# Forming the remainders of the down projection and of Wx on VectorE in place of GpSimd

## The chip, the cores and the metric

The kernel runs on one core of a Trainium2 chip. The metric is the device time of one execution in microseconds (us), lower is better. The engines of the core are TensorE (PE, and PEld for its weight loads), VectorE (DVE), ScalarE (ACT), GpSimd (POOL) and SyncE (SP), which here only issues transfers.

## The reference

Two layers, each added to its input. The first is a low-rank adaptation conditioned on `cond`; the second is a tanh recurrence over the time axis.

```
c   = layernorm(cond) * gamma + beta
w   = gelu(c @ W1 + bias1) @ W2 + bias2           # 16 x 16384
a1, b1, a2, b2 = split(w, 4)                      # each 16 x 512 x 8
u   = x . a2 ;  mid = gelu(x @ base_down + u . b2)
v   = mid . b1 ; out = mid @ base_up^T + v . a1
x   = x + (x + out)                               # B=16, T=512, D=512
xW  = x @ Wx + b
h_t = tanh(xW_t + h_{t-1} @ Wh)                   # h_0 = cond, 512 steps
y   = x + h
```

## The kernel before, in words

Matrix products of fp32 data are made from two rounded parts. A matrix W is held as `W[HI]`, W rounded to fp32r, and `W[LO]`, the remainder W - W[HI] rounded in turn; a product of two such matrices takes three passes (HI HI, HI LO, LO HI). ScalarE forms each HI part by a copy and another engine forms the LO part by a subtraction. For W2, up, x, mid and x1 that other engine is VectorE. For the down projection (`down_s`) and for Wx (`wx_s`) it is GpSimd (line L462): two instructions of 128x2048 elements in the whole kernel.

The work has three parts.

1. Start (about 0 to 28 us): layer norm, W1, the scale of Wh (`scl`), and the first weights. SyncE loads 1 MB pieces into a ring of four slots of the buffer `work`: entries 0 and 1 are up and down, entries 2 to 33 are the 32 half tiles of W2, entry 34 is Wx. Entry 4 waits until TensorE has turned up (`up_tr`), entry 5 goes into the slot of down and waits for `w_split` 1, the remainder of down. Entry e from 6 on waits until VectorE has formed the remainder of the W2 tile that lay in its slot (`w2_lo`). SyncE's queue is in order, and the loads of x for chunk 0 (`load_x`, L412) stand between entries 5 to 8.
2. Stream (about 28 to 176 us): `STREAM` = 39 steps written out by hand on each engine. In step i ScalarE rounds W2 tile i+2 (L489), VectorE forms the remainder of tile i (`w2_low`, L689), TensorE multiplies tile i with the hidden vector (L907), and the result is turned into the factors a1, b1, a2, b2. The tables `PE_FILL`, `ACT_FILL` and `DVE_FILL` put pieces of the first chunk's dense work between (`dense_slot(0, r)`).
3. Chunks: time is cut into 16 chunks of 32 steps. `chunk(c)` runs the recurrence (TensorE L944, VectorE L804 to L812, ScalarE L593) and interleaves the dense work of chunk c+1 and the first part of chunk c+2. Before chunk 0 the function `run_chunks` runs the last part of chunk 0's dense work: xw, the product with Wx, 48 matmuls of 512 columns in slots 24 to 31, together with the first part of chunk 1: VectorE transposes x (L728), ScalarE rounds it (L544), VectorE forms its remainder (L736).

The first xw matmul waits for `w_split` 2, the remainder of Wx (L995). The xw order takes for output tiles m=0 and m=1 first k = 0 to 2 (items 0 to 17), then k = 3 (from item 18). Item 0, 3, 6 and 18 wait for the remainder of x1 of k = 0, 1, 2, 3 (`x1lo_done`, VectorE L766), which follows `x1` (VectorE L761) and its rounding by ScalarE (L561). The first `down_s` matmul waits for `w_split` 1 (L962).

In VectorE's stream the second of these x1 (k=1) and the remainder k=0 stand in step 35, x1 of k=2 and the remainder of k=1 in step 36, the remainder of k=2 in step 37, x1 of k=3 in step 38. After the stream come the transposes of k=0 and k=1 of chunk 1, then the remainder of x1 k=3. ScalarE's order there is: x1 rounding k=0, Wx rounding (L583, step 35), x1 rounding k=1 and k=2, rounding of x k=0 and k=1 of chunk 1, x1 rounding k=3.

```
            for n, (src, dst) in enumerate(((down_f, down_s), (wx_f, wx_s))):
                pool.wait_ge(w_hi, n + 1)
                nc.gpsimd.tensor_tensor(dst[:, LO], src, dst[:, HI].bitcast(F32), ALU.subtract).then_inc(w_split, 1)
```

GpSimd's only other work behind these two is the sum of x1 and h, once per time step of the recurrence (L469).

Of the kernel before, what the change touches and what calls it, by code (L numbers as in the profile page):

```python
# [6 lines left out]
F32 = mybir.dt.float32  # L7
# [3 lines left out]
ALU = mybir.AluOpType  # L11
# [14 lines left out]
HI, LO = 0, 1  # L26
# [81 lines left out]
FIRST_TAIL = 24  # L108


WH_HI_AT, WH_LO_AT, WX_HI_AT = 0, 1, 35


def build(nc: bass.Bass, x, cond, down, up, gamma, beta, w1, bias1, w2, bias2, wx, wh, b, y):
# [13 lines left out]
    with ExitStack() as ctx:  # L128
        def sb(name, shape, dt=F32):
            return ctx.enter_context(nc.sbuf_tensor(name, shape, dt))  # L130
# [4 lines left out]
        def sem(name):  # L135
            return ctx.enter_context(nc.semaphore(name))


        down_s = sb("down_s", [P, 2, KT, D], F32R)
        up_s = sb("up_s", [P, 2, KT, D], F32R)  # L140
        wx_s = sb("wx_s", [P, 2, KT, D], F32R)
# [17 lines left out]
        up_f, down_f, wx_f = [work[:, s, :].rearrange("p (k n) -> p k n", k=KT) for s in range(3)]  # L159
# [76 lines left out]
        w_hi = sem("w_hi")  # L236
        w_split = sem("w_split")
# [112 lines left out]
        def plan(rank, first, shares):  # L350
            items = dense_items(KT, rank)
            parts = portions([1 if p >= 0 else 0.5 for _, _, p in items], shares)
            return stage_plan(items, {first + n: range(*part) for n, part in enumerate(parts)})
# [88 lines left out]
        @block.gpsimd  # L442
        def _(pool):
            nc.gpsimd.memset(ident[:], 0.0).then_inc(pool_set, 1)
            nc.gpsimd.memset(mask_b[:], 1.0).then_inc(pool_set, 1)
            pool.wait_ge(pool_set, 2)
            nc.gpsimd.affine_select(out=ident[:], in_=ident[:], compare_op=ALU.not_equal, fill=1.0, base=0,
                                    pattern=[[-1, P]], channel_multiplier=1).then_inc(pool_set, 1)

            for rep in range(REPS):  # L450
                m = mask_b[:, rep, :]
                base = -rep * GB * RANK
                nc.gpsimd.affine_select(out=m, in_=m, compare_op=ALU.is_ge, fill=0.0, base=base,
                                        pattern=[[-RANK, GB]], channel_multiplier=1).then_inc(pool_set, 1)
                pool.wait_ge(pool_set, 4 + 2 * rep)
                nc.gpsimd.affine_select(out=m, in_=m, compare_op=ALU.is_ge, fill=0.0, base=RANK - 1 - base,
                                        pattern=[[RANK, GB]], channel_multiplier=-1).then_inc(pool_set, 1)


            for n, (src, dst) in enumerate(((down_f, down_s), (wx_f, wx_s))):  # L460
                pool.wait_ge(w_hi, n + 1)
                nc.gpsimd.tensor_tensor(dst[:, LO], src, dst[:, HI].bitcast(F32), ALU.subtract).then_inc(w_split, 1)  # L462

            for c in range(NC):
                pool.wait_ge(x1lo_done, (c + 1) * KT)
                for t in range(TC):
                    pool.wait_ge(h_done, 2 * (c * TC + t) + 2)
                    xs = x1[c % 3].rearrange("p k (b t) -> p k b t", t=TC)[:, :, :, t]
                    nc.gpsimd.tensor_tensor(xs, xs, hf[:, t % 4], ALU.add).then_inc(sum_done, 1)  # L469
# [139 lines left out]
        def _(dve):  # L609
# [73 lines left out]
            def w2_low(n):  # L683

                dve.wait_ge(w2_hi, n + 1)
                if w2_prev[n] >= 0:
                    dve.wait_ge(row_mm, w2_prev[n] + 1)
                dst = w2_s[n].rearrange("p s k n -> p s (k n)")
                nc.vector.tensor_tensor(dst[:, LO], w2_raw(n), dst[:, HI].bitcast(F32),  # L689
                                        ALU.subtract).then_inc(w2_lo, 1)  # L690

            def split_up(k):

                src = bulk[:, BANK_UP[k], :]
                dve.wait_ge(up_hi, k + 1)
                nc.vector.tensor_tensor(up_s[:, LO, k], src, up_s[:, HI, k].bitcast(F32),
                                        ALU.subtract).then_inc(up_split, 1)

            def factor(n):

                q, dt = W2_TILES[n]
                f = fac[:, n % 2]
                dve.wait_ge(fac_mm, n + 1)
                if n == 0:
                    dve.wait_ge(small_in, 64)
                if n >= 2:
                    dve.wait_ge(fac_split, n - 1)
                nc.vector.tensor_reduce(fsum[:], rec[:, n % 2, 0:RANK * 2 * B].rearrange(
                    "p (r s b) -> p r b s", r=RANK, s=2), AX.X, ALU.add).then_inc(fsum_done, 1)
                dve.wait_ge(fsum_done, n + 1)  # L710
                pw = fsum[:].rearrange("p r (g b) -> p g b r", g=GROUPS)
                bias = bias2T[:, q, dt:dt + 1, :].rearrange("p (o a) r -> p o a r", o=1).broadcast_to([P, GROUPS, GB, RANK])
                for rep in range(REPS):
                    last = nc.vector.tensor_tensor(f[:, :, rep], pw, bias, ALU.add)
                last.then_inc(fac_done, 1)

            def split_factor(n):

                src, dst = factor_views(n)
                dve.wait_ge(fac_hi, n + 1)  # L720
                nc.vector.tensor_tensor(dst[:, LO], src, dst[:, HI].bitcast(F32), ALU.subtract).then_inc(fac_split, 1)
# [47 lines left out]
            def turn_y(c, k):  # L769

                if k == 0:
# [2 lines left out]
                nc.vector.transpose(yn[:, c % 2, :, k, :], x1[c % 3][:, k].rearrange(  # L774
                    "p (b t) -> p b t", t=TC)).then_inc(y_done, 1)

            for k in range(KT):
                split_up(k)
            for i in range(STREAM):
                if i < HALVES:  # L780
                    w2_low(i)
                if i % 2 == 0 and 0 <= i // 2 - 3 <= LAST:
                    split_factor(i // 2 - 3)
                if i % 2 == 0 and 0 <= i // 2 - 2 <= LAST:
                    factor(i // 2 - 2)
                if i == WH_LO_AT:
                    dve.wait_ge(wh_hi, 1)
                    nc.vector.scalar_tensor_tensor(out=wh_s[:, 1], in0=wh_f, scalar=w_scale, in1=wh_s[:, 0],
                                                   op0=ALU.mult, op1=ALU.subtract).then_inc(wh_split, 1)
                for r in DVE_FILL.get(i, ()):  # L790
                    dense_slot(0, r)

# [35 lines left out]
        def _(pe):  # L828
# [93 lines left out]
            def dense(stage_plan, i, banks, w_s, src, rank_f, done):  # L922

                items, _, starts, ends, _ = stage_plan
                m, k, p = items[i]
                if p >= 0:
                    a, w = PASSES[p]
                    mm = nc.tensor.matmul(bulk[:, banks[m], :], w_s[:, w, k, m * P:(m + 1) * P], src[:, a, k, :],  # L928
                                          start=(i in starts), stop=(i in ends), skip_group_check=True)
                else:  # L930
                    mm = nc.tensor.matmul(bulk[:, banks[m], k * GC:(k + 1) * GC],  # L931
                                          rank_f[:, -1 - p, k, m * P:(m + 1) * P], rank_s[:, k * GC:(k + 1) * GC],
                                          start=False, stop=(i in ends), skip_group_check=True)
                if i in ends:
                    mm.then_inc(done, 1)
# [125 lines left out]
```

## Time and profile before

| what | value |
|---|---|
| median of 3 runs | 1312.95 us (1311.94 to 1314.33) |
| the profiled execution | 1311.74 us |
| its span in the trace | 1310.0 us |
| TensorE | busy 1258.5 us, 96% of the span |
| VectorE, ScalarE, GpSimd busy | 990.0, 701.6, 288.9 us |
| mean granted TensorE clock | 0.972 of 2.4 GHz |

The span lies within the execution; 1.7 us of the profiled execution are outside it. Busy shares are averages over the three parts, which have different limits.

### The profile page before, as it was taken

The numbers are of one execution on the slowest core, as the hardware profiler recorded it, in microseconds if no ns is written. First come the engines' busy times: TensorE is split into PE (matmuls) and PEld (weight loads), VectorE is DVE, ScalarE is ACT, GpSimd is POOL, SyncE is SP. The second block draws the span as 40 slices with busy tenths as digits, with TensorE's granted clock in tenths as the row PEclk, the third lists the DMA queues.
The fourth block names the chain that finished last, engine by engine and source line by source line (L and its number), as shares of the span: only waits on it lengthen the run. The fifth ranks groups of instructions, "written<-read, shape, count | busy, mean of one in ns | idle before, by whom it ended". The sixth has DMA issues, their size and how long they took to land.

```text
span 1310.0 us, 49303 instructions
## 1 busy us (share of the span) xinstructions
PE 1258.5 (96%) x20280; PEld 1021.1 (78%) x20280; DVE 990.0 (76%) x3723; ACT 701.6 (54%) x2497; POOL 288.9 (22%) x525
## 2 busy tenths in 40 slices
PE   6698989999999999999999999999999999999996
PEld 6264578888888888888888888888888888888764
DVE  6679757777777878787878787777778787877664
ACT  4566635555555555555555555555555555555542
POOL 1000012222222222222222222222222222222111
PEclk6798889999999999999999999999999999999998
DMA  7888720121212122121312121212121221102022
GB/s 256 227 290 279 203 33 10 27 38 31 35 27 35 27 35 35 27 43 19 51 19 45 24 43 27 38 31 35 27 34 27 35 35 27 27 3 35 2 35 34
DMA packets 292271, 75.63 MB, mean 58 GB/s; under 512 B 273072, under 2 KB 273088, under 8 KB 292048
## 3 DMA queue, kind: packets, MB, share of 16 engines
q1 hardware_dynamic: 285680, 71.89, 24.7%
q8 instruction: 160, 2.62, 0.8%
q10 hardware_dynamic: 6368, 0.60, 0.4%
q14 instruction: 63, 0.52, 0.1%
HBM read 55.68 MB, written 16.78 MB: 55 GB/s over the span
## 4 chain that ended last, share of the span: by engine, by line
PE 85%; ACT 2%; DVE 2%; issue 0%; POOL 0%; DVEq 0%; POOLq 0%; ACTq 0%
PE bulk L928 43%; PE rec L944 31%; PE bulk L917 5%; PE bulk L931 5%; ACT hf L593 1%; PE bulk L907 1%; DVE z L804 1%; ACT rec L534 1%; PE rec L894 0%; POOL wx_s L462 0%; DVE work L774 0%; DVE wx_s L689 0%; ACT wx_s L583 0%; DVE hs L812 0%; DVE hs L809 0%
## 5 line engine op out<-in xcount | busy, mean ns | idle before, releaser
L944 PEld LDWEIGHTS rec<-hs,wh_s 128*128 128x128 f16 x16352 | 442.5, 96 | 129.0 <-DVE hs L812 126.4
L593 ACT ACTIVATE hf<-z,scl 128x32 f32<-128x32 f32 x1024 | 273.8, 315 | 482.4 <-DVE z L804 478.2
L944 PE MATMUL rec<-hs,wh_s 128*128 128x32 f16 x16352 | 493.2, 177 | 7.3 <-ACT rec L534 7.3
L469 POOL TENSOR_TENSOR work<-work,hf 128x64 f32<-128x64 f32 x512 | 278.4, 544 | 842.7 <-DVE hs L812 842.7
L804 DVE TENSOR_REDUCE z<-rec 128x32 f32<-128x96 f32 x1022 | 231.0, 256 | 111.1 <-PE rec L944 97.7
L809 DVE TENSOR_SCALAR hs<-hf 128x32 f16<-128x32 f32 x1024 | 181.5, 177 | 106.2 <-ACT hf L593 106.2
L812 DVE SCALAR_TENSOR_TENSOR hs<-hf,hs 128x32 f16<-128x32 f32 x1024 | 197.2, 193 | 35.3
L928 PE MATMUL bulk<-act_x,down_s 128*128 128x512 f32 x768 | 217.4, 406 | 2.1 <-ACT mid_s L556 2.1
L928 PE MATMUL bulk<-mid_s,up_s 128*128 128x512 f32 x768 | 218.8, 408 | 0.0
L928 PE MATMUL bulk<-act_s,wx_s 128*128 128x512 f32 x768 | 208.8, 409 | 3.5 <-POOL wx_s L462 3.5
L534 ACT ACTIVATE rec<-work 128x32 f32<-128x32 f32 x1022 | 183.7, 210 | 0.0
L928 PEld LDWEIGHTS bulk<-act_s,wx_s 128*128 128x128 f32 x768 | 136.7, 191 | 26.4 <-POOL wx_s L462 3.7
L928 PEld LDWEIGHTS bulk<-act_x,down_s 128*128 128x128 f32 x768 | 131.8, 188 | 20.4 <-ACT mid_s L556 2.3
L928 PEld LDWEIGHTS bulk<-mid_s,up_s 128*128 128x128 f32 x768 | 132.2, 189 | 17.6
L566 ACT ACTIVATE work<-bulk,bs,scl 128x512 f32<-128x512 f32 x64 | 48.1, 776 | 24.2 <-PE bulk L928 23.8
L728 DVE STREAM_TRANSPOSE work<-work 128x512 f32<-128x512 f32 x64 | 44.8, 703 | 7.5 <-DMA work<-in_x_dram 7.5
L766 DVE TENSOR_TENSOR act_s<-work,act_s 128x512 fp32r<-128x512 f32 x64 | 47.6, 745 | 1.9 <-ACT act_s L561 1.9
L931 PE MATMUL bulk<-rank_s,b_s 128*128 128x256 f32 x256 | 45.6, 292 | 0.0
L931 PE MATMUL bulk<-rank_s,a_s 128*128 128x256 f32 x256 | 45.6, 292 | 0.0
L757 DVE TENSOR_TENSOR mid_s<-gel,mid_s 128x512 fp32r<-128x512 f32 x64 | 43.8, 684 | 2.2 <-ACT mid_s L556 2.2
L761 DVE SCALAR_TENSOR_TENSOR work<-work,bulk 128x512 f32<-128x512 f32 x64 | 43.6, 681 | 2.3 <-PE bulk L931 0.9
L774 DVE STREAM_TRANSPOSE work<-work 128x512 f32<-128x512 f32 x64 | 44.7, 703 | 0.7 <-POOL work L469 0.5
(121 smaller groups left out, 971.4 us busy)
## 6 DMA issues: line engine op xcount, KB each, us to landing
work<-in_L_cond_W_dram SPq DMA_DIRECT2D x33, 1024.0 KB, 6.1
work<-in_x_dram SPq DMA_DIRECT2D x256, 64.0 KB, 3.4
out_dram<-work SPq DMA_DIRECT2D x248, 64.0 KB, 2.4
work<-in_L_cond_Wh_dram SPq DMA_DIRECT2D x1, 1024.0 KB, 5.4
work<-in_L_cond_base_up_dram SPq DMA_DIRECT2D x1, 1024.0 KB, 10.7
work<-in_L_cond_base_down_dram SPq DMA_DIRECT2D x1, 1024.0 KB, 13.2
work<-in_L_cond_Wx_dram SPq DMA_DIRECT2D x1, 1024.0 KB, 7.6
out_dram<-work ACTq DMA_DIRECT2D x8, 64.0 KB, 3.2
```

What stands on the lines that cost most here:

```text
L469: nc.gpsimd.tensor_tensor(xs, xs, hf[:, t % 4], ALU.add).then_inc(sum_done, 1)
L534: nc.scalar.activation(R[f][:, :, PARTS, :], xw[:, c % 2].rearrange("p k (b t) -> p k b t", t=TC)[:, f * HT:(f + 1) * HT, :, t], ACT.Copy) ...
L566: nc.scalar.activation(xw[:, n % 2, m], bulk[:, BANK_XW[m], :], ACT.Identity, bias=bs[:, m:m + 1], scale=fwd).then_inc(xw_done, 1)
L593: nc.scalar.activation(hf[:, t % 4, half], z[:, half], ACT.Tanh, scale=inv).then_inc(tanh_done, 1)
L766: nc.vector.tensor_tensor(act_s[:, LO, m], x1[n % 3][:, m], act_s[:, HI, m].bitcast(F32), ALU.subtract).then_inc(x1lo_done, 1)
L804: nc.vector.tensor_reduce(z[:, half], R[f].rearrange("p m j b -> p m b j"), AX.X, ALU.add).then_inc(z_done, 1)
L809: nc.vector.tensor_scalar(hs[:, half, 0, :], hf[:, t % 4, half], H_SCALE, None, ALU.mult).then_inc(hi_done, 1)
L812: nc.vector.scalar_tensor_tensor(out=hs[:, half, 1, :], in0=hf[:, t % 4, half], scalar=H_SCALE, in1=hs[:, half, 0, :], op0=ALU.mult, op1=A ...
L917: last = nc.tensor.matmul(bulk[:, out_bank, g * GC:(g + 1) * GC], fac_s[:, k, g, :], src[:, a, k, g * GC:(g + 1) * GC], start=(k == g == a ...
L928: mm = nc.tensor.matmul(bulk[:, banks[m], :], w_s[:, w, k, m * P:(m + 1) * P], src[:, a, k, :], start=(i in starts), stop=(i in ends), ski ...
L931: mm = nc.tensor.matmul(bulk[:, banks[m], k * GC:(k + 1) * GC], rank_f[:, -1 - p, k, m * P:(m + 1) * P], rank_s[:, k * GC:(k + 1) * GC], s ...
L944: last = nc.tensor.matmul(R[fo][:, m, 0:PARTS, :], wh_s[:, q, k, n * P:(n + 1) * P], hs[:, k, :, :], start=(m == k == q == 0), stop=(k == ...
```

## The change

GpSimd's loop over the two weights is taken out. VectorE gets the same two instructions. The one for down stands right before `split_up(0)`, so before the remainders of up and the whole stream; the one for Wx stands in step 36 of VectorE's stream (`WX_LO_AT`), behind the factor work of that step and ahead of x1 of k=2. Semaphores and their counts are unchanged.

```diff
-WH_HI_AT, WH_LO_AT, WX_HI_AT = 0, 1, 35
+WH_HI_AT, WH_LO_AT, WX_HI_AT, WX_LO_AT = 0, 1, 35, 36
...
-            for n, (src, dst) in enumerate(((down_f, down_s), (wx_f, wx_s))):
-                pool.wait_ge(w_hi, n + 1)
-                nc.gpsimd.tensor_tensor(dst[:, LO], src, dst[:, HI].bitcast(F32), ALU.subtract).then_inc(w_split, 1)
...
+            def split_weight(n, src, dst):
+
+                dve.wait_ge(w_hi, n + 1)
+                nc.vector.tensor_tensor(dst[:, LO], src, dst[:, HI].bitcast(F32), ALU.subtract).then_inc(w_split, 1)
+
+            split_weight(0, down_f, down_s)
             for k in range(KT):
                 split_up(k)
             for i in range(STREAM):
...
+                if i == WX_LO_AT:
+                    split_weight(1, wx_f, wx_s)
                 for r in DVE_FILL.get(i, ()):
                     dense_slot(0, r)
```

## Rows read from the trace of the kernel before

**Rows 1.** The page: the span, and the chain that ended last, by engine.

```profile
span 1310.0 us, 49303 instructions
...
PE 85%; ACT 2%; DVE 2%; issue 0%; POOL 0%; DVEq 0%; POOLq 0%; ACTq 0%
```

**Rows 2.** Stages: us, then busy time of each engine, clock, DMA share, GB/s.

```profile
240.00:1310.00 1070.00, 1053.07 (x18778) 877.93 (x18776) 817.51 (x3406) 570.78 (x2275) 267.58 (x492) 1.00 0.19 31
```

**Rows 3.** The chain that ended last, 172 to 193 us: start, us, what.

```profile
172.35 0.70 DVE work L761
...
173.69 1.82 ACT wx_s L583
175.58 4.53 POOL wx_s L462
180.15 12.46 PE bulk L928 x42
```

**Rows 4.** VectorE in order of time, 174 to 185 us (idle before in brackets).

```profile
174.66 0.68 DVE L761 SCALAR_TENSOR_TENSOR work<-work,bulk 128x512 f32<-128x512 f32 x1
176.05 5.19 DVE L766 TENSOR_TENSOR act_s<-work,act_s 128x512 fp32r<-128x512 f32 x2 [0.71 <-ACT act_s L561]
181.17 0.67 DVE L761 SCALAR_TENSOR_TENSOR work<-work,bulk 128x512 f32<-128x512 f32 x1
181.77 1.29 DVE L728 STREAM_TRANSPOSE work<-work 128x512 f32<-128x512 f32 x2
184.26 0.69 DVE L766 TENSOR_TENSOR act_s<-work,act_s 128x512 fp32r<-128x512 f32 x1 [1.21 <-ACT act_s L561]
```

**Rows 5.** VectorE in order of time, 21 to 54 us.

```profile
21.97 0.23 DVE L661 TENSOR_TENSOR h_s<-hT,h_s 128x64 fp32r<-128x64 f32 x1 [6.15 <-ACT h_s L496]
...
24.77 3.53 DVE L680 TENSOR_SCALAR z0s<-z0s,scl 128x64 f32<-128x64 f32 x1
...
28.35 2.47 DVE L696 TENSOR_TENSOR up_s<-bulk,up_s 128x512 fp32r<-128x512 f32 x4
...
53.64 0.71 DVE L728 STREAM_TRANSPOSE work<-work 128x512 f32<-128x512 f32 x1 [5.18 <-DMA work<-in_x_dram]
```

**Rows 6.** GpSimd in order of time, start of the kernel.

```profile
23.74 4.51 POOL L462 TENSOR_TENSOR down_s<-work,down_s 128x2048 fp32r<-128x2048 f32 x1 [21.35 <-ACT down_s L505]
```

**Rows 7.** Instructions on the tile wx_s: min/median/max ns, first and last start.

```profile
L689 DVE TENSOR_TENSOR wx_s<-work,wx_s x13: 2274/2284/2291, 39.8 to 159.4; 128x2048 fp32r<-128x2048 f32 x13
```

**Rows 8.** ScalarE in order of time, 26 us, and 175 to 184 us.

```profile
26.25 1.15 ACT L502 CAST up_s<-bulk 128x512 fp32r<-128x512 f32 x2
...
175.41 1.13 ACT L561 CAST act_s<-work 128x512 fp32r<-128x512 f32 x2
182.50 1.21 ACT L544 CAST act_x<-work 128x512 fp32r<-128x512 f32 x2 [5.96 <-DVE work L728]
183.62 0.61 ACT L561 CAST act_s<-work 128x512 fp32r<-128x512 f32 x1
```

**Rows 9.** SyncE's queue in order of time, 28 us.

```profile
28.69 3.29 SPq L412 DMA_DIRECT2D work<-in_x_dram  x4
```

**Rows 10.** Stage: us, clock, DMA share, GB/s.

```profile
28.00:30.00 2.00, 0.50 0.57 170
```

**Rows 11.** TensorE before the xw product, in order of time.

```profile
176.06 0.63 PE L931 MATMUL bulk<-rank_s,a_s 128*128 128x256 f32 x4
```

**Rows 12.** Stages, TensorE alone: us, busy (matmuls), clock, DMA share, GB/s.

```profile
180.15:185.80 5.65, 5.65 (x13) 0.50 0.13 21
185.80:192.40 6.60, 6.60 (x30) 1.00 0.63 100
```

**Rows 13.** Stages in and behind gaps of TensorE; columns as in rows 2.

```profile
126.00:128.06 2.06, 0.00 (x0) 0.00 (x0) 0.13 (x2) 2.06 (x5) 0.00 (x0) 1.00 1.00 368
142.70:145.19 2.49, 0.01 (x1) 0.01 (x1) 2.49 (x3) 1.03 (x2) 0.00 (x0) 0.93 0.66 249
145.20:148.26 3.06, 3.06 (x13) 1.67 (x14) 2.54 (x3) 2.57 (x3) 0.00 (x0) 0.50 0.63 172
```

## The prediction

> **What bounds the kernel now.** I read the page first, for its chain of work that ended last: 85% of it is TensorE [rows 1]. The stage view says where that holds: from 240 us to the end TensorE is busy 1053.07 of 1070 us at full clock [rows 2]. A change that touches nothing there moves the end by exactly as much as it moves the start of the recurrence, so the question is only what happens before the recurrence. There the chain in order of time has one place where TensorE is not the engine: ScalarE rounds Wx, GpSimd forms its remainder in 4.53 us, and the xw matmuls start as it ends, at 180.15 [rows 3]. TensorE's last matmuls before it end at 176.06 + 0.63 = 176.69 [rows 11], so it stands for 3.46 us.
>
> Next I read VectorE in order of time around both GpSimd instructions, looking for the same operation at another price. There are two. At 176.05 two remainders of 128x512 take 5.19 us together where the same operation takes 0.69 at 184.26; GpSimd works from 175.58 to 180.11 [rows 3, 4]. At 24.77 a scaling of 128x64 elements takes 3.53 us and ends at 28.30, where a subtraction of 128x64 takes 0.23; GpSimd's remainder of down ends at 23.74 + 4.51 = 28.25 [rows 5, 6]. I read both as VectorE held up until GpSimd's instruction is over. So each GpSimd instruction costs twice: its own length, and VectorE's time behind it.
>
> Last I read the granted clock. It is 0.50 from 180.15 to 185.80, in which 13 matmuls pass (0.43 us each), and 1.00 behind that, 30 to 31 in 6.60 us (0.213 each) [rows 12]. The fall came in the gap before 180.15: 1.2 GHz in place of 2.4.
>
> **The change, step by step.** The instruction itself is in the trace on VectorE: 13 remainders of the same shape, 2.28 us each [rows 7]. GpSimd's took 4.51 and 4.53 [rows 3, 6].
>
> *Down, at the start.* After the change VectorE's scaling at 24.77 finds GpSimd idle. I take 0.23 us, the 128x64 row; the ends are 0 and the 3.53 us of the row itself (rival C). With the small bias scaling behind it, priced at 0.1, VectorE is free at about 25.1. The remainder of down needs ScalarE's copy, done before 23.74 [rows 6], and runs from 25.1 to about 27.35. The remainders of up then start at 27.3 in place of 28.35 [rows 5]; ScalarE's last two copies of up end at 27.40 [rows 8] and the third remainder is not reached before 28.5, so nothing waits. Term: -1.05 us for everything behind VectorE: up, the first W2 remainders, the rows on TensorE, the scale of Wh.
>
> The second to wait for this is SyncE: entry 5 of the ring goes out with `w_split` 1, at 28.25 before [rows 6], the loads of x follow at 28.69 [rows 9]. It now goes at 27.35, 0.9 us earlier. Until 53.64 VectorE's transposes wait for these loads of x (5.18 us) [rows 5], so the term needs the transfers to move too. From 28 to 30 us the DMA engines are only 57% busy [rows 10]: they have room at the place where entry 5 arrives, so I take 0.9 to 1.05, call it 1.0. The other end is 0, if transfers set this part alone. From there to 174 us all engines wait for one another in the same order as before, and a shift carries through. TensorE's wait for `w_split` 1 at the first down matmul is long past. Nothing else stands in GpSimd's queue: its next work is the recurrence's sum.
>
> *Wx, at the end of the stream* (times of before, so without the shift). ScalarE's copy ends at 173.69 + 1.82 = 175.51 [rows 3]. VectorE reaches the new instruction at about 174.7, where x1 of k=2 began before [rows 4], stands 0.8 us, and runs it from 175.55 to 177.83. TensorE starts xw at 177.85, not 180.15: its gap is 1.16 us, not 3.46. Behind the new instruction in VectorE's queue stand x1 of k=2, the remainders of k=1 and k=2, x1 of k=3, two transposes and the remainder of k=3. With each at its row's price (0.68, 0.69, 0.67; starts follow 0.6 to 0.65 apart): x1 k=2 to 178.5, remainder k=1 to 179.1, ScalarE's copy of k=2 to 179.15, remainder k=2 to 179.85, x1 k=3 to 180.5. The transposes then start at 180.5 in place of 181.77, and from there to the end of the remainder k=3 it is 184.26 + 0.69 - 181.77 = 3.18 us, through ScalarE's three copies [rows 4, 8]: done at 183.7 in place of 184.95.
>
> TensorE: items 0 to 2 at 0.213 to 178.5; 0.6 us for k=1; items 3 to 5 to 179.8; items 6 to 17 from 179.9 to 182.45; 1.25 us for k=3; item 18 at 183.7. Before: 5.65 us at 0.43 is 13.2 items by 185.80, 4.8 more at 0.213 make 18 items at 186.8 [rows 12], later than the 184.95 at which k=3 was ready; the slow clock set it. Term: 183.7 - 186.8 = -3.1 us, if the clock stays up. Of this, 1.25 is the earlier remainder k=3 and 1.85 is the clock. Does it stay? A gap of 2.06 us passed with the clock at 1.00, one of 2.49 was followed by 0.50 [rows 13]. The new gaps are 1.16, 0.6, 0.1 and 1.25 us with work between. The nearest row is the one that stayed. If the clock falls all the same at about 180.1, 11 items at 0.43 end at 184.8, and some 2 us more at half speed cost 1.0: the term is -1.1. All that follows (the rest of xw, the first z) waits for TensorE, not for VectorE, whose work for chunk 1 ends 1.25 us earlier as well.
>
> **The sum.** -1.0 - 3.1 = -4.1 us against the profiled execution's 1311.74, so 1307.6. The median of the runs is 1312.95, 1.2 above that execution; nothing in the terms depends on which execution it is but the place where the clock changes. I predict the median: 1312.95 - 4.1 = 1308.8 us, 0.32% faster. A measurement of this kernel can tell about 0.2% (2.6 us) from no change.
>
> **The rivals.**
> *A, the clock falls in the split gap too.* For it: the row at 2.49 us, and the several waits within 6 us that together make 3.1. Against: the row at 2.06 and work between the waits. -1.0 - 1.1 = -2.1: 1310.8, within 0.2%.
> *B, the start gives nothing.* Transfers set the time to 53.64, and the ones of x keep their pace. For: the wait of 5.18 us; against: 57% at 28 to 30 us. -3.1 alone: 1309.8, just over 0.2% faster.
> *C, slower: VectorE's long instructions are long of themselves.* The 3.53 and the 5.19 us would then stay, and 2.28 us come on top. Start: the remainders of up begin at 30.6, +2.25. End: x1 k=2 to 178.5, the pair to 183.7, x1 k=3 to 184.3, transposes from there, remainder k=3 at 187.5, item 18 at 187.5 instead of 186.8, +0.7. Sum +2.95: 1315.9. It decides from the point where more than 2.3 us of the 3.53 are the instruction's own. Against: two different operations end with or right after GpSimd's, and the second has a row at 0.69.
> The Trainium skill, page "SBUF — State Buffer", section "Who interferes with whom", speaks to C: a VectorE instruction with two SBUF inputs, or in a two-port mode, and a GpSimd instruction exclude each other for the whole instruction, and the one that comes second is blocked. By that rule both long rows are waits and C falls; the trace agrees, with ends at 28.30 against 28.25. The same rule would speak against the change if GpSimd had other work beside the new instructions; it has none there.
> *D, before had less clock to lose.* Where the gap of 3.46 us leaves the clock up in the runs without a profile, the gain is -1.0 - 1.25 = -2.3: 1310.7.
>
> **Chances.** Forecast 0.62 (1307.3 to 1310.0 with the scatter of the runs shown, 1.2 us), B 0.14, A 0.12, D 0.08, C 0.04. Faster by over 0.2% (under 1310.3): most of the forecast, two thirds of B and a little of A and D, 0.71. Slower: C, 0.04. Within: 0.25. The range reaches from the forecast less the scatter and the earlier end of the terms, 1306.4, to A and D with some scatter, 1311.5.
>
> **What would show it.** VectorE's scaling at 24.8 at 0.2 to 0.3 us and no instruction of 128x512 over 1 us; the first up remainder about 1.05 us earlier; the last transposes of x at about 52.6; a TensorE gap of about 1.2 us before xw and three short waits in its first 18 items; clock 1.00 from there on; the first z of the recurrence about 4 us earlier than before, and the same length from there to the end. The prediction is wrong if the clock is 0.50 behind the gap, if the shift of the start is gone by 174 us, or if the span behind the first z changes.

## The result, and the profile after

The changed kernel takes 1308.87 us (median of 9 runs, 1307.43 to 1310.93); the kernel before, in 9 runs with it, 1314.62 us. The ratio is 0.9962, 95% interval 0.9952 to 0.9972: 5.0 us faster, between 3.7 and 6.3. The forecast was 4.1 us faster and 1308.8 us. The median of before shown ahead of the forecast (1312.95, three runs) lay 1.7 us under the later one. So the forecast of the time itself is met to 0.1 us by luck: the base was 1.7 us low and the gain 0.9 us small. What is to be compared is 4.1 with 5.0.

The profiled execution takes 1308.32 us. From its page, with rows 1 to compare:

```profile
span 1306.6 us, 49303 instructions
```

Start of VectorE's stream in the changed kernel, in order of time (compare [rows 5]):

```profile
25.89 0.16 DVE L675 COPY scl<-rec 128x3 f32<-128x3 f32 x1 [0.71 <-PE rec L880]
26.09 0.25 DVE L676 TENSOR_SCALAR z0s<-z0s,scl 128x64 f32<-128x64 f32 x1
...
26.39 2.29 DVE L776 TENSOR_TENSOR down_s<-work,down_s 128x2048 fp32r<-128x2048 f32 x1
28.59 2.48 DVE L692 TENSOR_TENSOR up_s<-bulk,up_s 128x512 fp32r<-128x512 f32 x4
...
54.13 0.71 DVE L724 STREAM_TRANSPOSE work<-work 128x512 f32<-128x512 f32 x1 [5.05 <-DMA work<-in_x_dram]
```

The scaling that took 3.53 us takes 0.25, the remainder of down 2.29. The first remainder of up starts 2.70 us after the copy of `scl`; before it was 28.35 - 24.58 = 3.77. That is 1.07 us less, where the forecast had 1.05. This execution is 1.3 us later than before at that copy, and the change is not the reason (last section), so times are counted from that copy from here on.

The chain that ended last, 172 to 190 us (compare [rows 3]):

```profile
172.67 0.70 DVE work L757
...
173.40 0.62 ACT act_s L557
174.02 1.82 ACT wx_s L579
...
175.86 2.29 DVE wx_s L776
178.15 0.61 DVE work L757
...
178.79 0.63 ACT act_s L557
...
179.44 0.69 DVE act_s L762
180.13 0.60 DVE work L757
180.73 0.64 DVE work L724
...
181.39 1.21 ACT act_x L540 x2
182.60 0.53 ACT act_s L557
...
183.15 0.70 DVE act_s L762
...
183.90 5.73 PE bulk L932 x24
```

Before, the chain went from GpSimd straight into 42 matmuls. Now the remainder of Wx is 2.29 us of it and the chain stays in VectorE's queue behind it: x1 of k=2, the remainder of k=2, x1 of k=3, the first transpose, ScalarE's three copies, the remainder of k=3. Only at item 18 does it enter TensorE. The lines left out are waits of at most 0.04 us. These are the steps of the forecast in their order.

TensorE there, and its stages (compare [rows 11, 12]):

```profile
176.40 0.63 PE L935 MATMUL bulk<-rank_s,a_s 128*128 128x256 f32 x4
178.21 0.96 PE L932 MATMUL bulk<-act_s,wx_s 128*128 128x512 f32 x3 [1.18 <-DVE wx_s L776]
179.41 3.79 PE L932 MATMUL bulk<-act_s,wx_s 128*128 128x512 f32 x15 [0.24 <-DVE act_s L762]
183.90 5.73 PE L932 MATMUL bulk<-act_s,wx_s 128*128 128x512 f32 x24 [0.69 <-DVE act_s L762]
```

```profile
178.20:183.90 5.70, 4.76 (x19) 1.00 0.08 13
183.90:189.60 5.70, 5.70 (x26) 1.00 0.63 100
```

The gap is 1.18 us in place of 3.46, the clock stays at 1.00 (2.4 GHz) through it and the small waits behind it, and the 24 matmuls from 183.90 on take 5.57 us, 0.23 each.

### The profile page after: what moved, and what is told of

It reads as the page before. It is cut to its first block, busy times and chain, and to the rows that moved or that the text cites. A ratio compares the mean times of both kernels' runs of the same rounds, so it can differ in the third digit from the quotient of the medians.

```text
span 1306.6 us, 49303 instructions
## 1 busy us (share of the span) xinstructions
PE 1257.4 (96%) x20280; PEld 1020.0 (78%) x20280; DVE 987.6 (76%) x3725; ACT 701.6 (54%) x2497; POOL 280.0 (21%) x523
## 4 chain that ended last, share of the span: by engine, by line
PE 90%; DVE 4%; ACT 3%; DMA 1%; issue 1%; SPq 0%; ACTq 0%; DVEq 0%; POOLq 0%; POOL 0%
PE bulk L932 43%; PE rec L948 31%; PE bulk L921 5%; PE bulk L935 5%; PE bulk L911 3%; ACT hf L589 1%; PE rec L898 1%; DVE act_s L685 1%; DVE z L808 1%; DMA work<-in_L_cond_W_dram 1%; ACT rec L530 1%; DVE wx_s L685 1%; PE rec L849 1%; PE bulk L867 1%; DMA work<-in_x_dram 0%
## 5 line engine op out<-in xcount | busy, mean ns | idle before, releaser
L562 ACT ACTIVATE work<-bulk,bs,scl 128x512 f32<-128x512 f32 x64 | 48.0, 775 | 22.1 <-PE bulk L932 21.8
L762 DVE TENSOR_TENSOR act_s<-work,act_s 128x512 fp32r<-128x512 f32 x64 | 43.8, 684 | 1.3 <-ACT act_s L557 1.2
```

The lines of the kernel that those rows point to most:

```text
L562: nc.scalar.activation(xw[:, n % 2, m], bulk[:, BANK_XW[m], :], ACT.Identity, bias=bs[:, m:m + 1], scale=fwd).then_inc(xw_done, 1)
```

## The experiments

One table holds what the traces say of all kernels, in us. The columns: from the copy of `scl` to the first remainder of up; from that copy to VectorE's fourth transpose of x, the last wait for transfers of the start; from that transpose to x1 of k=0; from there to the first z of the recurrence; from there to the end of the span. Then the ratio to the kernel before, run beside each of them, with its 95% interval.

| kernel | scl to up | scl to 4th transpose | to x1 | x1 to z | z to end | ratio |
|---|---|---|---|---|---|---|
| before | 3.77 | 29.06 | 118.71 | 23.93 | 1113.72 | 1 |
| changed | 2.70 | 28.24 | 118.54 | 20.63 | 1113.30 | 0.9962 (0.9952 to 0.9972) |
| e1 down only | 2.70 | 28.61 | 119.31 | 23.81 | 1114.08 | 0.9998 (0.9989 to 1.0007) |
| e2 Wx only | 3.79 | 28.85 | 122.04 | 20.64 | 1114.01 | 0.9976 (0.9966 to 0.9987) |
| e3 filled gap | 4.23 | 29.58 | 116.85 | 22.16 | 1114.22 | 0.9983 (0.9972 to 0.9995) |
| e4 Wx twice | 2.70 | 28.10 | 118.91 | 23.97 | 1113.39 | 0.9983 (0.9975 to 0.9992) |
| e5 GpSimd beside | 3.80 | 31.66 | 119.42 | 25.89 | 1113.89 | 1.0031 (1.0019 to 1.0043) |
| e6 x1 first | 2.69 | 28.16 | 118.92 | 19.86 | 1113.75 | 0.9955 (0.9943 to 0.9967) |
| e7 Wx early | 2.70 | 28.28 | 121.15 | 18.73 | 1113.76 | 0.9955 (0.9943 to 0.9967) |
| e8 changed again | 2.69 | 28.16 | 118.78 | 20.63 | 1113.34 | 0.9961 (0.9948 to 0.9973) |
| e9 down thrice | 7.35 | 33.28 | 121.05 | 20.62 | 1113.41 | 1.0010 (1.0001 to 1.0019) |
| e10 entry 5 late | 2.69 | 30.68 | 120.98 | 20.62 | 1113.92 | 0.9992 (0.9983 to 1.0000) |
| e11 down early | 0.50 | 28.52 | 118.73 | 20.63 | 1113.46 | 0.9973 (0.9964 to 0.9983) |
| e12 both early | 0.50 | 28.86 | 119.40 | 18.68 | 1113.74 | 0.9963 (0.9950 to 0.9977) |

The two rows of before that the table needs and that do not stand above, in VectorE's order of time:

```profile
24.58 0.16 DVE L679 COPY scl<-rec 128x3 f32<-128x3 f32 x1 [0.70 <-PE rec L876]
...
196.28 0.35 DVE L800 TENSOR_TENSOR z<-z0s,work 128x32 f32<-128x32 f32 x2 [7.73 <-ACT work L566]
```

The column x1 to z repeats to 0.01 us between kernels that have the same code there (20.62 to 20.64 in six of them). The column to x1 does not: 116.9 to 122.0 with the same code (e7 and e12 alone differ there, at its end). A microsecond is therefore read from its stage, and the ratios say only whether it arrived.

**e1, down alone.** The Wx loop stays on GpSimd:

```diff
-                if i == WX_LO_AT:
-                    split_weight(1, wx_f, wx_s)
...
+            pool.wait_ge(w_hi, 2)
+            nc.gpsimd.tensor_tensor(wx_s[:, LO], wx_f, wx_s[:, HI].bitcast(F32), ALU.subtract).then_inc(w_split, 1)
```

> Only the remainder of down is formed by VectorE; the remainder of Wx stays on GpSimd. The theory (GpSimd's instruction holds VectorE up, so VectorE's 2.28 us in place of 3.3 us of waiting gains 1.05 us, carried by the transfers): VectorE's scaling of 128x64 takes 0.25 us, the stretch from the copy of scl to x1 of k=0 is 1.0 us shorter than before, and the time is 1.0 us under the kernel before. The xw end is as before: the pair of remainders of k=1 and k=2 over 5 us, a TensorE gap of 3.4 us, the clock at 0.50 behind it. Rival, transfers set this part: 0 us. Rival, the 3.53 us are the scaling's own: 2.2 us more than before.

VectorE's part of the start is 1.07 us shorter, the end is as before (23.81). The expected 1.0 us at x1 of k=0 was missed: the fourth transpose is 0.45 us earlier (28.61 against 29.06), and x1, counted from the copy of `scl`, comes 147.92 us behind it where before had 147.77. The time is 0.3 us under before, between 1.4 under and 0.9 over. That holds the forecast's 1.0 and also zero: neither the time nor x1 settles this part. The 2.2 us more of the rival are excluded.

**e2, Wx alone.** The reverse: `split_weight(0, ...)` is taken out and GpSimd forms the remainder of down.

> Only the remainder of Wx is formed by VectorE; the remainder of down stays on GpSimd. The theory: the scaling of 128x64 stays at about 3.5 us, the start as before; the stretch from x1 of k=0 to the first z of the recurrence 3.3 us shorter than before (20.6 in place of 23.9), the clock at 1.00 there, and the time 3.1 to 3.7 us under the kernel before. Rival, the two parts need one another (a gain that shows only with both): under 2 us here.

As expected: the stage is 20.64, the time 3.2 us under before (1.7 to 4.5). The scaling of 128x64 is long again, in VectorE's order of time of this kernel:

```profile
26.06 3.55 DVE L679 TENSOR_SCALAR z0s<-z0s,scl 128x64 f32<-128x64 f32 x1
```

**e3, the gap filled.** The kernel before; TensorE does 14 matmuls of no use while GpSimd forms the remainder of Wx:

```diff
                 for r in PE_FILL.get(i, ()):
                     dense_slot(0, r)
+            for j in range(14):
+                nc.tensor.matmul(bulk[:, BANK_IDLE, :], up_s[:, HI, 0, 0:P], mid_s[:, HI, j % KT, :],
+                                 start=True, stop=True)
```

> The kernel before, with 14 matmuls of 512 columns on TensorE between the end of the stream and the xw product (their result is not used), about 3.0 us of work inside the gap of 3.46 us; GpSimd forms both remainders as before. The theory (1.85 us of the term for Wx is the slow clock behind the gap): the clock stays at 1.00, TensorE's item 18 waits for the remainder of k=3 as it is ready 8.3 us after the start of that part, and the stretch from x1 of k=0 to the first z is 1.8 us shorter than before (22.1). Rival, the whole gain is the earlier start of TensorE and of VectorE's queue, the clock being of no weight: 0 us or longer by what the extra matmuls delay.

TensorE in order of time, and its stages:

```profile
176.11 3.36 PE L1013 MATMUL bulk<-mid_s,up_s 128*128 128x512 f32 x14
179.81 4.42 PE L928 MATMUL bulk<-act_s,wx_s 128*128 128x512 f32 x18 [0.34 <-POOL wx_s L462]
184.67 5.73 PE L928 MATMUL bulk<-act_s,wx_s 128*128 128x512 f32 x24 [0.45 <-DVE act_s L766]
```

```profile
175.00:180.00 5.00, 4.66 (x23) 1.00 0.00 0
180.00:184.00 4.00, 4.00 (x18) 1.00 0.05 8
```

The 18 items take 4.42 us, item 18 waits for the remainder of k=3, and the stage is 22.16 where 22.1 was expected and 23.93 stood before. So 1.77 us of the stage's 3.30 are the slow clock: GpSimd's work ends no earlier (0.1 us later, counted from x1 of k=0), and TensorE has more matmuls to do. The whole kernel is 2.2 us faster than before (0.7 to 3.7).

**e4, Wx twice.** The changed kernel with the subtraction for Wx done a second time in front of the first:

```diff
                 if i == WX_LO_AT:
+                    dve.wait_ge(w_hi, 2)
+                    nc.vector.tensor_tensor(wx_s[:, LO], wx_f, wx_s[:, HI].bitcast(F32), ALU.subtract).then_inc(twice, 1)
+                    dve.wait_ge(twice, 1)
                     split_weight(1, wx_f, wx_s)
```

> The changed kernel with the remainder of Wx formed twice by VectorE, 2.28 us more in front of the xw product. The theory: TensorE's gap becomes 3.4 to 3.5 us, the clock falls to 0.50 in it, and the 18 first items, not the remainder of k=3, decide again: 3.2 to 3.8 us over the changed kernel, so about as slow as the kernel before in this part. Rival, only the length counts: 2.2 us over the changed kernel, with the clock at 1.00.

Its stages, TensorE alone:

```profile
177.30:180.80 3.50, 0.00 (x0) 0.83 0.00 0
180.80:186.40 5.60, 5.60 (x13) 0.50 0.07 12
```

2.28 us of work cost 3.34 us of the stage (23.97 against 20.63): the gap is 3.5 us again and 13 matmuls take 5.6. The clock comes back as a cost as soon as the gap does, whichever engine makes it.

**e5, GpSimd beside.** The changed kernel; GpSimd does both subtractions as well, in halves, into a buffer of its own, and SyncE's entry 5 waits for the first two halves:

```diff
                     sp.wait_ge(w_split, 1)
+                    sp.wait_ge(spare_done, 2)
...
+            for n, (src, dst) in enumerate(((down_f, down_s), (wx_f, wx_s))):
+                pool.wait_ge(w_hi, n + 1)
+                for h in range(2):
+                    half = slice(h * HT, (h + 1) * HT)
+                    pool.wait_ge(spare_done, 2 * n + h)
+                    nc.gpsimd.tensor_tensor(spare[:], src[:, half], dst[:, HI, half].bitcast(F32),
+                                            ALU.subtract).then_inc(spare_done, 1)
```

> The changed kernel, and beside it GpSimd forms the same two remainders once more into a spare buffer that nobody uses, each in two halves of 1024 columns; the transfer of ring entry 5 waits for the first of them too. The theory (a GpSimd instruction holds VectorE up for its length): the scaling of 128x64 behind it takes 2 us or more again in place of 0.25, the remainder of down comes out late, and the start is 2 to 3.5 us longer; at the end of the stream the instructions of the two engines take turns, the remainder of Wx is 2.2 to 4.5 us late, the clock falls to 0.50; in all 4 to 8 us over the changed kernel. Rival, the two engines run side by side and the 3.53 and 5.19 us had other causes: under 1 us.

VectorE, GpSimd and TensorE in order of time:

```profile
26.24 1.35 DVE L689 TENSOR_SCALAR z0s<-z0s,scl 128x64 f32<-128x64 f32 x1
...
29.84 2.47 DVE L705 TENSOR_TENSOR up_s<-bulk,up_s 128x512 fp32r<-128x512 f32 x4
...
180.31 2.29 DVE L789 TENSOR_TENSOR wx_s<-work,wx_s 128x2048 fp32r<-128x2048 f32 x1 [0.79 <-ACT wx_s L592]
182.52 0.68 DVE L770 SCALAR_TENSOR_TENSOR work<-work,bulk 128x512 f32<-128x512 f32 x1
183.11 5.02 DVE L775 TENSOR_TENSOR act_s<-work,act_s 128x512 fp32r<-128x512 f32 x2
```

```profile
25.19 6.97 POOL L468 TENSOR_TENSOR spare<-work,down_s 128x1024 fp32r<-128x1024 f32 x2 [22.82 <-ACT down_s L512]
...
180.35 7.24 POOL L468 TENSOR_TENSOR spare<-work,wx_s 128x1024 fp32r<-128x1024 f32 x2 [148.18 <-ACT wx_s L592]
```

```profile
182.65 0.98 PE L945 MATMUL bulk<-act_s,wx_s 128*128 128x512 f32 x3 [1.18 <-DVE wx_s L789]
185.43 0.97 PE L945 MATMUL bulk<-act_s,wx_s 128*128 128x512 f32 x3 [1.80 <-DVE act_s L775]
```

The holding goes both ways. VectorE's remainder of Wx began 0.04 us before GpSimd's instruction and took its usual 2.29; GpSimd's two halves took 7.24, where the whole took 4.53 before, 2.71 more. Behind it VectorE's pair took 5.02 in place of 1.46. The scaling took 1.35, less than the 2 expected: it waited for GpSimd's first half only. This work of no use cost 9.1 us over the changed kernel (1.0031 against 0.9962), more than the 8 expected. I had the remainder of Wx as the one held up; it was the pair behind it, and the stage grew by 5.3 us. The start grew by 3.4; this follows from the added wait of entry 5, since GpSimd's first two halves end at 32.16 and x is loaded from 32.67 on, not 29.11.

The page "SBUF — State Buffer" of the Trainium skill, section "Who interferes with whom", says of VectorE's two-port modes that whoever issues first has the shared pair for its whole instruction. The trace shows the same for subtractions with both inputs in SBUF, 2.29 for the first and 7.24 for the second.

Not every VectorE instruction is held. The remainders of up and x1 of k=2 have one input in PSUM (`bulk`); beside GpSimd's work they took 2.47 and 0.68 us, as in the changed kernel (2.48 and 0.68).

TensorE's clock fell here too. Its gaps were 1.18, 1.80 and 1.80 us, with three matmuls (about 1 us) between them; the mean clock was 1.00 from 184 to 186 us, 0.79 from 186 to 188, and 0.50 from 188 to 190. So splitting a gap does not by itself keep the clock.

**e6, x1 first.** In the changed kernel the remainder of Wx goes behind x1 of k=2:

```diff
-                if i == WX_LO_AT:
-                    split_weight(1, wx_f, wx_s)
...
                                                    op1=ALU.add).then_inc(x1_done, 1)
+                if n == 0 and r == 20:
+                    dve.wait_ge(w_hi, 2)
+                    nc.vector.tensor_tensor(wx_s[:, LO], wx_f, wx_s[:, HI].bitcast(F32), ALU.subtract).then_inc(w_split, 1)
```

> The changed kernel with x1 of k=2 ahead of the remainder of Wx in VectorE's step 36, in the 0.8 us in which VectorE waits there for ScalarE's copy. The theory (VectorE's queue behind the remainder of Wx sets TensorE's item 18): everything behind the remainder of Wx is 0.65 us earlier, the two short waits of TensorE in the first 18 items are gone, the stretch from x1 of k=0 to the first z is 20.0 us in place of 20.6. Rival, TensorE's start alone sets it: 0.

The stage is 19.86 (20.0 expected), 0.77 less. VectorE's queue behind the remainder sets item 18, not TensorE's start: the gap before xw is 1.19 us as in the changed kernel. The ratio's 0.9 us under the changed kernel lies inside the intervals.

**e7, Wx early.** ScalarE's copy in step 32 (`WX_HI_AT` = 32), VectorE's remainder in four parts of 512 columns, called `wx_piece`:

```diff
+                if i == 34:
+                    wx_piece(0)
                 if i % 2 == 0 and 0 <= i // 2 - 2 <= LAST:
                     factor(i // 2 - 2)
...
+                if i == 34:
+                    wx_piece(1)
...
+                if n == 0 and r == 20:
+                    wx_piece(2)
+                    wx_piece(3).then_inc(w_split, 1)
```

> The changed kernel with ScalarE's copy of Wx in its step 32, where ScalarE waits, and VectorE's remainder of Wx in four parts of 512 columns: two in step 34, where VectorE waits, two in step 36 behind x1 of k=2. The theory: the remainder is ready as the stream ends, TensorE has no gap before xw, the remainder of k=3 comes about 1.9 us earlier, the stretch from x1 of k=0 to the first z is 18.7 us in place of 20.6, the clock stays at 1.00. Rival, the parts in step 34 delay the last factor and x1 of k=0 by what they save behind it: 0.

The stage is 18.73, as expected to 0.03 us; TensorE has no gap before xw. The rival is out: from TensorE's matmuls of the last W2 tile held in `wx_s` to x1 of k=0 it is 9.31 us (165.60 to 174.91), in e8 9.30 (163.73 to 173.03), so the parts in step 34 delay nothing. Still the ratio, 0.9955, is the same as that of e6 and not told apart from that of the changed kernel.

**e8, the changed kernel again,** beside e5 to e7.

> The changed kernel itself, beside the three others. The theory: 0.32% to 0.38% under the kernel before, as 1.0 us of the start and 3.3 us of the end; the scaling 0.25 us, the stretch from x1 of k=0 to the first z 20.6 us, the clock at 1.00 through the gap.

5.1 us under before (3.5 to 6.8). All stages repeat to 0.25 us.

**e9, down thrice.** Two more subtractions of down, each waiting for the one before it, ahead of `split_weight(0, ...)`.

> The changed kernel with the remainder of down formed three times by VectorE, 4.6 us more in front of the remainders of up and of the release of ring entry 5. The theory (a shift of this point carries through transfers and stream to the end): VectorE's fourth transpose of x, 28.25 us behind the copy of scl in the changed kernel, comes 4.3 to 4.7 us later, and the time is about 4.5 us over the changed kernel, so within 1 us of the kernel before. Rival, the transfers or the stream swallow a shift: under 2 us.

The fourth transpose comes 5.0 us later (33.28), where 4.3 to 4.7 were expected, and the whole 6.3 us over the changed kernel (1.0010 against 0.9962), where 4.5 were. Nothing swallows a delay of the start. The stretch to x1 is 2.5 us longer too; whether that follows from the delay is open (last section).

**e10, entry 5 late.** VectorE as in the changed kernel; SyncE waits longer:

```diff
                     sp.wait_ge(w_split, 1)
+                    sp.wait_ge(up_split, KT)
```

> The changed kernel in which SyncE sends ring entry 5, and with it the queue of x behind, only when the remainders of up are formed too, about 2.4 us later; VectorE's work is not touched. If the transfers carry the shift of the start, as the argument with the wait of the transposes says: the fourth transpose 2.0 to 2.4 us later than in the changed kernel, the time about 2 us over it. If VectorE's own queue carries it: nothing up to 0.5 us.

The transpose comes 2.44 us later, the time is 3.9 us over the changed kernel, where 2 were expected; the stretch to x1 is 2.4 us longer as well. VectorE's remainders of up are where they were (2.69), so a later release alone delays the transfers and, through them, the transpose.

**e11, down early.** Copy and remainder of down go to where ScalarE and VectorE stand still, before the hidden vector:

```diff
+            arrived(act, DOWN_ENTRY)
+            nc.scalar.copy(down_s[:, HI], down_f).then_inc(w_hi, 1)
             act.wait_ge(hT_mm, 1)
             act.wait_ge(vT_done, 1)
...
-            arrived(act, DOWN_ENTRY)
-            nc.scalar.copy(down_s[:, HI], down_f).then_inc(w_hi, 1)
...
             link(nc.vector.tensor_copy(z0s[:], Z0))
+            dve.wait_ge(w_hi, 1)
+            nc.vector.tensor_tensor(down_s[:, LO], down_f, down_s[:, HI].bitcast(F32), ALU.subtract).then_inc(w_split, 1)
...
-            split_weight(0, down_f, down_s)
```

> The changed kernel with ScalarE's copy of down ahead of the hidden vector (ScalarE stands still for 15 us there) and VectorE's remainder of down ahead of the wait for it (VectorE stands still for 6 us). The theory: both leave the path, the remainders of up begin 2.2 us earlier after the copy of scl, entry 5 goes out right behind entry 4, the fourth transpose comes 2.2 to 2.7 us earlier, and the time is 2 us under the changed kernel. Rival, down arrives too late for it: 0 or slower.

The theory fell. VectorE's work is 2.2 us earlier (0.50 in place of 2.70) and entry 5 goes out with entry 4, about 2.8 us earlier, but the fourth transpose stays (28.52 against 28.24), and the kernel is 1.4 us slower than the changed one by the ratios, whose intervals just overlap. SyncE's queue in e11 and the stages of both (clock, DMA share, GB/s):

```profile
25.34 0.92 SPq L407 DMA_DIRECT2D work<-in_L_cond_W_dram  x2
26.30 6.16 SPq L412 DMA_DIRECT2D work<-in_x_dram  x4
```

```profile
28.00:30.00 2.00, 1.00 1.00 348
```

The changed kernel's queue, and the same stage:

```profile
25.38 3.69 SPq L407 DMA_DIRECT2D work<-in_L_cond_W_dram  x2
29.11 3.06 SPq L412 DMA_DIRECT2D work<-in_x_dram  x4
```

```profile
28.00:30.00 2.00, 0.78 0.97 343
```

The room in the transfers that stood there before (57% [rows 10]) is used up by the change itself (97%). Before was 1.3 us earlier in this part, so e2, whose copy of `scl` is at 25.86, is the fairer comparison: its DMA share falls to 0.38 from 30 to 31 us, where the changed kernel has 0.98. Issuing still earlier makes the issues of the first x loads last 6.16 us instead of 3.06, and SyncE's lead is gone later: the second x loads go out at 35.04 and 35.13, the third at 41.23 and 41.09.

**e12, both early.** e7 and e11 together.

> The early down of e11 and the early Wx of e7 together. The theory: the two add, 2.2 us and 1.9 us, 4 us under the changed kernel and 9 us under the kernel before; the stretch from x1 of k=0 to the first z 18.7 us. Rival, the parts of Wx in step 34 stretch the stream by what they save: 2 us under the changed kernel.

The stage x1 to z is 18.68, the start as in e11 (28.86 to the fourth transpose); 4.9 us under before where 9 were expected, no better than the changed kernel. As in e7, the parts in step 34 stretch nothing behind them, so neither the theory nor the rival accounts for the whole.

## Why the prediction was right

**GpSimd's instruction costs twice.** Shown by e2 and e5: VectorE's small scaling is 0.25 us when GpSimd is idle, 3.53 and 3.55 when it works, 1.35 when it works in halves. Rival C, that the instructions are long of themselves, is out. It holds for the instructions with all their data in SBUF; e5 shows two kinds, with an input in PSUM, that were not held.

**The start, -1.0.** VectorE gained its 1.07. At the fourth transpose, counted from the copy of `scl`, the three traces with GpSimd's remainder of down in its place (before, e2, e3) give 29.06, 28.85 and 29.58, the six with VectorE's alone (changed, e1, e4, e6, e7, e8) 28.10 to 28.61, on average 28.26: 0.9 less. In e3 the copy of `scl` came 0.45 us earlier beside ScalarE's copy of down, which GpSimd waits for; without that the difference is 0.75. The path is the one of the forecast as far as a delay goes: releasing entry 5 later (e10) delays the transpose by 2.44. An earlier release than the change's own gives nothing (e11), so the room that the forecast read from the 57% was just enough for its term. That the gain arrives at the end was not shown for itself: the pair before and changed has x1 0.99 us earlier (147.77 and 146.78 behind the copy), e1 has it 0.15 later, and e1's interval holds both 1.0 and zero. Rival B's 3.1 for the whole lies under the measured 3.7 to 6.3, yet it is not excluded as a statement on the start alone; e9 and e10, which carry delays in full and more, make it unlikely.

**Wx, -3.1.** Measured 3.30 in the stage (23.93 to 20.63), and 3.29 in e2. Its parts: 1.77 clock (e3) against 1.85 forecast; the rest 1.53, against 1.25. Of the 0.2 in all, 0.12 lie in the steps behind the remainder: item 18 starts 183.90 - 172.67 = 11.23 us after x1 of k=0, the working had 183.7 - 172.35 = 11.35. The other 0.08 lie in before, where item 18 was only worked out, at 186.8: with the 9.40 us that z follows item 18 in the changed kernel it would be 196.28 - 9.40 = 186.88. One price was too low, the 0.213 us of a matmul at the full clock: the measured 0.23 and more made the waits in the first 18 items 0.24 and 0.69 us where the working had 0.6, 0.1 and 1.25. It changed nothing, as item 18 waits for the remainder of k=3 either way.

**The clock stays up.** Gaps of 1.18, 0.24 and 0.69 us left it at 1.00 in all six traces with these gaps (changed, e2, e8 to e11); e4's gap of 3.5 us lost it, and so did e5's split gap of 1.18, 1.80 and 1.80. Rival A did not occur, but e5 shows that its mechanism is real at gaps not much longer. The forecast took the nearest single gap as its row, and no row stood there for several gaps in a row; this step was a judgement that came out. Rival A's own sum is 0.1 us off: 184.8 + 1.0 - 186.8 is -1.0, not -1.1. Rival D says that before sometimes keeps the clock; before was traced once, and e1, which has the same end, lost it too (stage 23.81). D's whole gain of 2.3 lies under the measured interval.

**The sum.** The stages give 0.8 to 0.9 and 3.3, so 4.1 to 4.2 us; the runs 5.0 (3.7 to 6.3). The 0.8 or 0.9 between them is inside the interval; I have no cause to put it to. The forecast had named a change of the stretch behind the first z as a sign of being wrong. There the two traces differ by 0.42 us (1113.72 and 1113.30), but all fourteen lie between 1113.30 and 1114.22, e1 to e3 above before, and kernels with the change up to 1113.92. So no change there is shown, and 0.4 us cannot be excluded.

## What to carry to other kernels

A long elementwise instruction on GpSimd beside VectorE is not free just because GpSimd is idle otherwise: look at what VectorE's next instructions take while it runs, and compare with the same instruction elsewhere in the trace. When a gap of TensorE is cut, read the granted clock behind it as well as the gap: here 1.8 of the 5.0 us were matmuls at 2.4 GHz that had run at 1.2. Cutting a gap into pieces is no guarantee: pieces of up to 1.2 us kept the clock, pieces of up to 1.8 us lost it. And when a shift rests on transfers having room, the room bounds it: the first 0.9 us of an earlier release were worth nearly their length at the fourth transpose, the next 2.8 us nothing.

## What was not expected

The part between the fourth transpose and x1 took 116.9 to 122.0 us in kernels that are identical there (e7 and e12 but for its end, where they lose nothing). The long ones (e2, e7, e9, e10: 121.0 to 122.0) have TensorE at 0.50 from 60 to 68 us; of the others only e5, with 119.42, has it from 60 to 64. e2, then the changed kernel, by stages:

```profile
60.00:64.00 4.00, 3.19 (x8) 0.77 (x6) 4.00 (x4) 3.22 (x5) 0.00 (x0) 0.50 0.76 233
64.00:68.00 4.00, 4.00 (x16) 2.14 (x17) 3.97 (x6) 2.38 (x2) 0.00 (x0) 0.50 0.94 302
```

```profile
60.00:64.00 4.00, 2.87 (x15) 1.49 (x14) 4.00 (x4) 3.98 (x6) 0.00 (x0) 0.91 0.74 229
64.00:68.00 4.00, 4.00 (x13) 2.17 (x12) 3.97 (x6) 1.99 (x3) 0.00 (x0) 0.67 0.95 307
```

This stretch alone could make the scatter of before's own runs, 1311.94 to 1315.15 us, which is larger than the start term. It may be why e9 and e10 lost more (6.3, 3.9) than their transposes (5.0, 2.4); whether a later start makes this slow stretch likelier, or those two executions merely met it, the single traces do not say. Nor do they say why e7 and e12, 1.9 us shorter in their stage, are not faster by as much.

Of the 1.3 us by which the changed kernel's trace was later at the copy of `scl`, 0.2 stand before the first matmuls of Wh and 1.1 come from them, 16 at a time, in order of time before and after:

```profile
7.04 2.48 PE L845 MATMUL rec<-h0T,work 128*128 128x16 f32 x16
```

```profile
7.24 3.60 PE L849 MATMUL rec<-h0T,work 128*128 128x16 f32 x16
```

The change does not reach this place, and it is not the cause: e9 and e10, which contain it, take 2.54 and 2.37 us there, the changed kernel and the ten others with an edit 3.6. In the three traces with the short time (before, e9, e10) the granted clock falls between 8 and 9 us and is 0.50 from 9 to 20; in the eleven others it is 1.00. What sets this is open. Without it the span would have shrunk by 4.7 us instead of 3.4.
